# Router logits computed token by token in a two-layer mixture-of-experts and attention kernel

## The reference

```
# one feed-forward layer, on the layer-normalised x
logits = x @ router_w + router_b                 # [tokens, 8]
topk_vals, topk_idx = top_k(logits, 2)
full_w = sum(one_hot(topk_idx) * softmax(topk_vals))
h = x @ expert_w[e] + expert_b[e]                # for the 8 experts, all computed
combined = sum_e full_w[:, e] * silu(h_e)
out = combined @ proj_w + proj_b
y = x + out
return norm_w * y / sqrt(mean(y * y) + 1e-6)
# the whole: x = x + 0.5 * ffn(ln(x)); x = x + attn(ln(x)); x = x + 0.5 * ffn(ln(x))
```

## Time and profile before

| | us |
|---|---|
| median of three runs | 827.2 |
| lowest, highest | 824.89, 829.65 |
| profiled execution, first to last instruction (span) | 825.8 |
| TensorE matmuls busy | 792.3 (96%) |
| weight loads busy | 697.7 (84%) |
| VectorE busy | 651.9 (79%) |
| ScalarE busy | 507.4 (61%) |
| GpSimd busy | 517.2 (63%) |

### The profile page before, as it was taken

The page is one execution under the profiler, slowest core; times in us unless marked ns, Lnnn a source line. Parts: engine busy times, 40 slices in busy tenths (PEclk is TensorE's granted clock), DMA queues, the critical chain, the costliest instruction groups (busy, mean ns, idle before and its releaser), DMA issues.

```text
span 825.8 us, 16045 instructions
## 1 busy us (share of the span) xinstructions
PE 792.3 (96%) x4712; PEld 697.7 (84%) x4712; DVE 651.9 (79%) x1917; ACT 507.4 (61%) x1250; POOL 517.2 (63%) x408
## 2 busy tenths in 40 slices
PE   7899999859999999999999999999999999999996
PEld 4688878658999999999899998999999988788885
DVE  6988996886677686786866868768687799988876
ACT  3565565567667586675765767557576586444543
POOL 4636648693878778787777777877878761112302
PEclk9999999978999999999999999999999999999998
DMA  9245412201132122212312313132131110000001
GB/s 295 86 135 191 148 58 52 52 13 39 27 77 73 41 51 76 51 25 64 102 26 50 88 30 85 27 88 51 31 96 25 39 27 1 1 1 26 2 26 52
DMA packets 28998, 50.09 MB, mean 61 GB/s; under 512 B 3874, under 2 KB 9634, under 8 KB 28962
## 3 DMA queue, kind: packets, MB, share of 16 engines
q1 hardware_dynamic: 28964, 49.67, 21.5%
HBM read 18.72 MB, written 9.96 MB: 35 GB/s over the span
## 4 chain that ended last, share of the span: by engine, by line
PE 82%; DVE 6%; POOL 5%; ACT 3%; issue 2%; DMA 1%; SPq 0%; POOLq 0%; DVEq 0%; ACTq 0%
PE pt L1696 8%; PE pj L1631 5%; PE pj L1633 5%; PE pj L1632 5%; PE o L1710 5%; PE o L1711 4%; PE o L1712 4%; PE sc L1685 4%; PE sc L1684 4%; PE sc L1683 4%; PE pj L1740 4%; PE pj L1742 3%; PE pj L1741 3%; PE sc L973 3%; PE sc L975 3%; PE sc L974 3%
## 5 line engine op out<-in xcount | busy, mean ns | idle before, releaser
L1260 POOL TENSOR_TENSOR at_ql<-at_rot,at_qh 128x512 fp32r<-128x512 f32 x64 | 82.7, 1292 | 103.0 <-ACT at_qh L1485 102.9
L1387 DVE TENSOR_TENSOR at_ptl<-pt,at_pth 128x512 fp32r<-128x512 f32 (+1 forms) x192 | 108.9, 595 | 45.9 <-ACT at_pth L1532 45.6
L1532 ACT ACTIVATE at_pth<-pt 128x512 fp32r<-128x512 f32 (+1 forms) x192 | 94.0, 525 | 81.9 <-PE pt L1696 81.9
L1526 ACT ACTIVATE at_pr<-at_pr,at_low 128x512 f32<-128x512 f32 (+3 forms) x256 | 140.5, 557 | 3.0 <-DVE at_low L1373 2.9
L1272 POOL TENSOR_TENSOR at_rot<-at_rot,gc 128x512 f32<-128x512 f32 x80 | 103.3, 1291 | 6.3
L1382 DVE TENSOR_SCALAR at_pr<-at_pr,at_inv 128x128 f32<-128x128 f32 (+3 forms) x256 | 105.3, 473 | 2.3
L1268 POOL TENSOR_TENSOR at_rot<-ga,cos 128x512 f32<-128x512 f32 x80 | 104.5, 1307 | 2.3 <-POOL at_ql L1260 2.3
L1270 POOL TENSOR_TENSOR gc<-gc,sin 128x512 f32<-128x512 f32 x80 | 103.9, 1299 | 1.0 <-DMA gc<-ga 1.0
L1373 DVE CUSTOM_DVE_ANT_0 at_pr<-sc,at_mask 128x512 f32<-128x512 f32 (+2 forms) x192 | 100.8, 549 | 0.4 <-PE sc L1685 0.3
L1696 PE MATMUL pt<-ident,at_pr 128*128 128x128 f32 x640 | 93.6, 277 | 6.8 <-DVE at_ptl L1387 5.1
L1485 ACT ACTIVATE at_qh<-at_rot 128x512 fp32r<-128x512 f32 x64 | 40.6, 634 | 95.9 <-POOL at_rot L1272 95.9
(11 more groups left out here) (282 smaller groups left out, 2263.6 us busy)
## 6 DMA issues: line engine op xcount, KB each, us to landing
gc<-ga SPq DMA_DIRECT2D x160, 128.0 KB, 2.3
ga<-in_attn_w SPq DMA_DIRECT2D x8, 384.0 KB, 4.8
gb<-attn_split SPq DMA_DIRECT2D x6, 512.0 KB, 4.2
at_wo<-attn_split SPq DMA_DIRECT2D x6, 512.0 KB, 4.3
attn_split<-gb SPq DMA_DIRECT2D x6, 384.0 KB, 2.4
attn_split<-gc SPq DMA_DIRECT2D x6, 384.0 KB, 3.3
x<-in_x SPq DMA_DIRECT2D x4, 512.0 KB, 9.3
e_raw<-in_expert_w SPq DMA_DIRECT2D x8, 256.0 KB, 6.2
```

Of the source, the lines that this page charges most:

```text
L1387: dve.tensor_tensor(ptl[h % 2][:, cols], pt[(NF * h + k) % 2][:, 0:FLEN[k]], pth[h % 2][:, cols].bitcast(F32), ALU.subtract).then_inc(lo_d ...
L1526: act.activation(pr[h % 2][:, cols], pr[h % 2][:, cols], ACT.Exp, bias=low[h % 2][:, i:i + 1], scale=-1.0, accum_out=tot[h % 2][:, i:i + 1 ...
```

## The change

The roles in the router's product are exchanged. The tokens become stationary, a tile of 128 at a time, and the router's columns move: 16 (leading and rest) against `zh`, and the 8 leading ones against `zl`. Per block there are four tiles by two chunks by two matmuls, sixteen in all, each with a weight load of its own. The result has its tokens on the partitions at once, at the same columns of the bank at which `choose` read it before. `logits_out`, `logits_back`, the zeroed wide operands and their two memsets, and one small cast go. `router` signals `tb_done` itself. The space that `r_hl` and `r_h0` took stays reserved, so no other tile moves.

```diff
@@ vector, first layer only
-                dve.memset(r_hl[:].bitcast(F32), 0.0).then_inc(setup, 1)
-                dve.memset(r_h0[:].bitcast(F32), 0.0).then_inc(setup, 1)
                 norm_stats(0)
                 norm_rows(0)
                 shift_pair(0)
                 dve.wait_ge(cols_in, 16)
-                dve.wait_ge(setup, 2)
                 dve.tensor_copy(r_hl[:, :, 0:E], r_raw).then_inc(r_split, 1)
-                dve.tensor_copy(r_h0[:, :, 0:E], r_raw).then_inc(r_split, 1)
-                dve.wait_ge(r_split, 2)
+                dve.wait_ge(r_split, 1)
@@ scalar
-            def logits_out(j):
-                act.wait_ge(rout_done, j + 1)
-                act.activation(rT[:], t_ps[1][:], ACT.Copy).then_inc(rT_done, 1)
...
-                if i < LAST:
-                    logits_out(i + 1)
...
-            logits_out(0)
@@ tensor
             def router(j):
                 if first or j > 0:
                     pe.wait_ge(zlo_done, C * (j - J0) + C)
-                b = slice(j * SEQ, (j + 1) * SEQ)
-                for c in range(C):
-                    pe.matmul(t_ps[1][:], r_hl[:, c, :], zh[:, c, b], start=(c == 0), stop=False)
-                    r = pe.matmul(t_ps[1][:], r_h0[:, c, :], zl[:, c, b], start=False, stop=(c == C - 1))
-                r.then_inc(rout_done, 1)
-
-            def logits_back(j):
-                pe.wait_ge(rT_done, j + 1)
                 for t in range(BT):
-                    r = pe.transpose(t_ps[1][:, t * P:(t + 1) * P], rT[:, t * P:(t + 1) * P], ident[:])
+                    tok = slice(j * SEQ + t * P, j * SEQ + (t + 1) * P)
+                    for c in range(C):
+                        pe.matmul(t_ps[1][:, t * P:t * P + 2 * E], zh[:, c, tok], r_hl[:, c, :], start=(c == 0), stop=False)
+                        r = pe.matmul(t_ps[1][:, t * P:t * P + E], zl[:, c, tok], r_hl[:, c, 0:E], start=False, stop=(c == C - 1))
                 r.then_inc(tb_done, 1)
...
                 sum_T(i, 0)
-                if i < LAST:
-                    logits_back(i + 1)
-                elif first:
+                if first and i == LAST:
                     step_project(0)
...
                 row_of(3)
-                logits_back(0)
```

## The result

The changed kernel takes **834.1 us** (median of 4 runs, 833.21 to 834.85) against 826.8 of the kernel before, run beside it. The ratio is 1.0093, with a 95% interval of 1.0077 to 1.0108: slower by 0.93%, or about 7 us. The forecast was 830.6 us, with a range of 825.5 to 836.5. The sign of the sum was right and the time is inside the range. But it lies outside the 828.5 to 833 that the forecast gave its own case, and the class held likeliest, within 0.5%, did not come: +3.4 us became about +7.4.

A forecast was written before the change was run, and what follows sets the result against it. TensorE's work, 82% of the chain that ended last, was taken to bound the kernel. Six steady routers +2.3, first start +0.8 and second start +0.3 us made +3.4 on 827.2, so 830.6 us, range 825.5 to 836.5.

The forecast's parts named there:

- its own case: Whole kernel: the forecast's sum of +3.4 us holds, 828.5 to 833 us; chance 0.62.
- the class held likeliest: Whole kernel: change within about 0.5%, 4.1 us, of no change; chance 0.53.
- rival 2: Clock falls at routers in the loops, 1.7 us each; with three falls +8.5 us, 836 us; chance 0.14.
- Load-paced pairs: Each narrow router matmul costs the next one's weight load, 0.11 us, however few its columns; sixteen cost 1.76 us.
- Rivals 1 and 3: Router pairs: fast loads of 0.06 us, 823.9 us, chance 0.10; no overlap, 0.19 us each, 841 us, chance 0.06.
- The steady term: Six routers inside the loops: 1.76 us comes, 1.37 goes, +0.39 us each, +2.3 us in all.
- rival 4: Loops: extra time hidden in TensorE's waits, steady term near 0.5, total about 828.5 us; chance 0.08.
- The second start: Router ahead of the second layer's loop: +0.83 us on TensorE, VectorE waits 0.3 us, so +0.3 us.
- The first start: Router ahead of the first layer's loop, at 1.2 GHz: +0.8 us taken, bounds +0.2 and +1.9.
- if it rises at the same moment: First start: TensorE's clock rises at the same moment, so twelve expert matmuls end about 0.2 us later.
- if it stays low until they are done: First start: clock low until the twelve expert matmuls end, at 23.06 against 21.1 us, +1.9 us.
- rival 3: No overlap of loads: 0.19 us a pair, steady +10.0, first start 5.3 - 2.76, 841 us; chance 0.06.

The follow-up runs named there:

- h2: The unchanged kernel before, profiled a second time ("before, again"); 826.08 us.
- h1: The changed kernel, unaltered, run and profiled once more ("after, again (1)"), against the kernel before; 833.24 us, ratio 1.0089.
- Experiment 4: Changed kernel with eight fillers ahead of the first half block's last expert pair, beside the changed kernel again; 831.02 against 833.24 us.
- e2: Kernel before with the new router only ahead of the first layer's loop, against the kernel before; 827.11 us, ratio 1.0008.
- e3: The change with each of the sixteen router matmuls moving 128 columns instead of 16 or 8, against the kernel before; 833.34 us, ratio 1.0085.
- g1: Changed kernel plus eight filler matmuls ahead of the last expert pair of the first half block, against the kernel before; 831.02 us, ratio 1.0069.
- h3: The unaltered changed kernel, profiled a third time ("after, again (2)"); 835.80 us.
- experiment 3: Same filler matmuls at both starts and the attention's start, in the kernel before and the changed kernel; 828.54 and 830.21 us.
- e1: The change everywhere except ahead of the first layer's loop, where the old router stays, against the kernel before; 830.67 us, ratio 1.0060.
- e4: The change without the product with z's low part, so eight pairs a router, against the kernel before; 825.12 us, ratio 0.9985.
- f1: Kernel before plus filler matmuls at the start, first half block and attention's start, against the kernel before; 828.54 us, ratio 1.0017.

## Why the prediction was right, and where it was not

The direction and the mechanism of the loops came as forecast. That the time fell inside the range is in part luck: the range reached to 836.5 to leave room for a fall of the clock in the loops (rival 2), and what filled that room was the clock at the first start and in the attention.

**Load-paced pairs: right.** 0.11 us a pair was taken from the earlier trace rows; measured 0.112 with 8, 16 and 128 columns and with 8 or 16 pairs. A fixed cost of each matmul doesn't explain it, since the first two start 0.03 us apart, and at half clock a pair takes 0.21. One reading was off without harm: a load starts 0.05 us to 0.08 us (above) behind the matmul before it, not with it. Rivals 1 and 3 fall. The figure of about 81 ns a pair in the Trainium skill, page "TensorE: Matmul & The Clock Gate", section "Back-to-back issue gap", is not seen here; the measured 0.112 us decides.

**The steady term: right in kind, a little small.** Forecast +0.39 each, measured +1.34 to +1.55 a layer for three, 0.45 to 0.52 each. The router itself gives 1.80 - 0.93 = 0.87, the transposes -0.44, together 0.43. The rest, in layer 1, are the dozen or two expert matmuls behind a router: 0.231 us apart where it is 0.227 otherwise, some 0.05 to 0.09 us in all. Why they are slower I can't say. Six make +2.9 in place of +2.3.

**Hidden elsewhere (rival 4): wrong as a rival.** TensorE's waits from 31 to 125 us after, beside the earlier trace rows:

```profile
PE sc L957 <- DVE f_e_lo L474: 2.1, 1, 2.1
PE pt L971 <- DVE f_acc L494: 0.8, 2, 0.4
```

From 26 us on there is one more, of 1.3 us ahead of the first of these. It belongs to the first start and is in the second trace of before too. The loops had nothing to give back, and gave nothing.

**The second start: right.** +0.3 was forecast from the earlier trace rows; VectorE now waits 0.30 us where it didn't (timeline of VectorE), and the segment is longer by 0.42 to 0.49.

```profile
710.31 0.69 DVE L1387 TENSOR_TENSOR x<-pj,x 128x512 f32<-128x512 f32 x1 [0.30 <-PE pj L1722]
```

**The first start: the step that was mis-sized.** It said "if it rises at the same moment" +0.2 and "if it stays low until they are done" +1.9, and took +0.8. That it can pass on at all through SiLU, tanh and GpSimd is what the traces show. But the mean of three traces of after is 37.4 us and that of two of before 34.7: +2.7, and single pairs give +0.35 to +4.45. Three things made the difference.

- The shift of the experts' start. +0.32 was worked out, with 17.58 - 12.49 - 2.00 = 3.09 us going from the old start; rival 3 had 2.76 for the same. By the timelines the transposes hold the experts back by 17.23 - 16.47 = 0.76 us and not by the 1.04 of the chain, and the experts start 0.80 later. At an equal rise most of this is regained, since more of the twelve matmuls then run at 0.23: the twelfth starts at 21.78 us in h2 (rise at 21.5) and at 22.16 in h1 (21.4), and the loop's first router at 35.08 and 35.43. That is +0.35 where the sum had +0.2.
- The rise itself. The sum counted from the one trace at hand, which rose at 19.4 us; the same kernel also rises at 21.5, the changed one at 21.4 to 24.6. Between the first traces of before and after (19.4 and 23.4) the twelfth matmul moves from 20.82 to 22.89 us and GpSimd's residual by 2.2 us, about the +1.9 of the upper bound.
- A fall behind the wait for the split weights, which the sum had at nothing. The earlier trace rows shows full clock behind that same wait of 2.2 us, and I took this as a reason against a fall anywhere. In two of three traces of after the clock falls there. These two rose latest, so TensorE had the least time at full clock ahead of the wait; that is an order seen in five traces, and no test of a cause. Experiment 4 takes the fall away and gains 1.6 us in its trace.

What sets the moment of the rise is not shown. The new first start is also in e2 and e3, which rose at 21.6 and 20.9 us and have starts of 35.52 and 35.30; e2's own time went up by 0.9 us only. So the +2.7 of three traces may be more than the first start costs on average.

**The clock (rival 2): right that it matters, wrong in place.** Both loops are at 1.00, so no router makes it fall. But a fall costs what was worked out, 1.7 us (1.6 in one pair of traces), and it came at the first start.

**Not in the prediction: the attention.** No instruction of it is changed but those of layer 2's start behind it; it only begins later. A third stretch at half clock there goes with about 2 us more and is present in all three traces of after, but not in g1's.

The account of the traces' means, 832.4 against 825.0 or +7.5 (medians: +7.4): routers in the loops +2.9, second start +0.45, first start +2.7, attention +1.0 (563.4 in the mean against 562.5), end of the kernel +0.45 (h1 and h3 have 0.7 us more behind the last expert matmul, where the clock fell earlier). It closes because it is made of differences of the same traces; with three and two of them, only the first two terms are the same in every pair. They come to +3.4, which is the forecast's whole sum and near the 2.6 to 3.3 us of experiment 3.

**Left open.** What fixes the phase of the clock's changes, and so whether a given delay costs once or twice. Why the whole costs some 2 us more than e1 and e2 together. No version here is faster than the kernel before by more than its interval: e4 (0.9985) comes near, but leaves a product out.

## What to carry to other kernels

A matmul whose stationary tile is new cost its load here, 0.112 us at full clock, with 8, 16 or 128 moving columns: 4 matmuls of 512 columns became 16 of 16 or 8, which saved nearly all columns and made four times the loads, and the loads decided. And where a kernel has stretches in which TensorE's clock comes and goes, take more than one trace of it before and after: one execution says where the clock rose that time, and the same start here was 35.4, 38.0 and 38.7 us long.

## What the hardware showed that was not expected

- The clock fell while TensorE was busy. In f1 it had risen to 2.4 GHz at 5.2 us, among 24 filler instructions, and fell at 8.6 us, although TensorE was busy for all of the 3.4 us between (the row of experiment 3), more than half of it with bias matmuls that contract over 2 rows. It then stayed at 0.50 for 17.1 us, with matmuls busy for 16.53 of them, among them expert matmuls over all 128 rows. No run shows whether the few rows were the reason.
- The spacing of loads is 0.112 us under 8, 16 and 128 moving columns alike, while each load's own row says 0.19.
- A delay of 1.6 us in the first layer cost 3.6 us, and one of 1.85 us in the second 2.0 (medians, with overlapping intervals): behind the first there is still the attention, whose clock falls two or three times.
